# Moving small table steps, two weight loads and one VectorE step inside the first layer norm of a GNN and expert kernel

## The reference

```
def _sage_layer(h, edge_src, edge_dst, deg_inv, W_self, W_neigh, b):
    msg = h[edge_src]
    agg = segment_sum(msg, edge_dst, num_segments=h.shape[0])
    mean = agg * deg_inv[:, None]
    return h @ W_self + mean @ W_neigh + b

def gnn(x):                       # x is already layer-normed
    h = relu(_sage_layer(x, ..., W_self0, W_neigh0, b0))
    return _sage_layer(h, ..., W_self1, W_neigh1, b1)

def ffn(t):                       # t is already layer-normed
    logits = silu(t @ rw1 + rb1) @ rw2 + rb2          # 8 experts
    w = softmax(top 2 of logits, the rest -inf)
    eh = silu(einsum('td,edh->teh', t, ew1) + eb1)    # hidden size 256
    return t + einsum('te,ted->td', w, einsum('teh,ehd->ted', eh, ew2) + eb2)

x = x + gnn(layernorm(x))
x = x + ffn(layernorm(x))
```

## Time and profile before

| | |
|---|---|
| median of 3 runs | 1164.46 us (1163.42 to 1165.69) |
| the profiled execution, its own time | 1165.69 us |
| its span (first to last instruction) | 1163.9 us |
| PE busy | 1083.5 us, 93% |
| DVE busy | 627.1 us, 54% |
| ACT busy | 434.5 us, 37% |
| POOL busy | 177.0 us, 15% |
| PE on the chain that ended last | 75% of the span |

### The profile page before, as it was taken

How to read it: one execution, slowest core, us unless ns; L and a number is a source line. 1 busy time by engine, 2 the same in 40 slices (tenths; PEclk the granted TensorE clock), 3 DMA queues, 4 the chain that set the end, 5 groups by cost and what they waited for, 6 DMA issues and landing times.

```text
span 1163.9 us, 18112 instructions
## 1 busy us (share of the span) xinstructions
PE 1083.5 (93%) x6504; PEld 1025.4 (88%) x6504; DVE 627.1 (54%) x1099; ACT 434.5 (37%) x936; POOL 177.0 (15%) x199
## 2 busy tenths in 40 slices
PE   4999999999989999999999999999993699999984
PEld 3999999999989999999999999999993598888883
DVE  6578888888452542234224432642215567777752
ACT  5554434444111221121211121643322556667651
POOL 5500000000000020002000200024511223443211
PEclk9999999999999999999999999999996699999977
DMA  7332223321328530033003401765641779999963
GB/s 190 82 103 76 64 68 104 103 72 60 106 57 246 161 101 1 1 128 95 1 1 127 119 1 36 228 195 160 187 172 42 275 245 307 263 271 254 243 173 55
DMA packets 73659, 150.45 MB, mean 129 GB/s; under 512 B 12347, under 2 KB 51192, under 8 KB 69074
## 3 DMA queue, kind: packets, MB, share of 16 engines
q1 hardware_dynamic: 61041, 112.50, 31.0%
q0 software_dynamic: 11840, 36.22, 12.5%
q10 hardware_dynamic: 672, 0.32, 0.1%
HBM read 109.97 MB, written 44.53 MB: 133 GB/s over the span
## 4 chain that ended last, share of the span: by engine, by line
PE 75%; DVE 7%; DMA 5%; issue 4%; ACT 3%; PEld 2%; DVEq 1%; ACTq 1%; POOL 0%; POOLq 0%; SPq 0%; PEldq 0%
PE ps L1459 19%; PE ps L936 14%; PE ps L1531 9%; PE ps L1498 8%; PE ps L1190 7%; PE ps L2087 5%; DMA out<-o_rows,to_i 4%; PE ps L808 4%; PE ps L2103 2%; DVE w_lo L2169 2%; PE ps L2073 1%; ACT w_hi L2123 1%; PEld ps L732 1%; DVE o_rows L2191 1%; PE ps L904 1%
## 5 line engine op out<-in xcount | busy, mean ns | idle before, releaser
L1421 POOL TENSOR_TENSOR s_rows<-s_rows,b1t 125x1368 f32<-125x1368 f32 (+3 forms) x9 | 23.1, 2584 | 584.1 <-DMA s_rows<-in_x 584.1
L815 DVE TENSOR_TENSOR adj<-ps,adj 125x250 f32 x212 | 88.2, 416 | 41.7 <-PE ps L808 33.3
L936 PE MATMUL ps<-h_lo,w_hi 128*128 128x418 f32 x336 | 108.6, 372 | 0.0
L936 PE MATMUL ps<-h_hi,w_hi 128*128 128x418 f32 x336 | 100.3, 379 | 0.0
L1498 PE MATMUL ps<-z_lo,adj 125*125 125x342 f32 (+1 forms) x300 | 95.4, 323 | 2.3 <-issue 2.3
L1498 PE MATMUL ps<-z_hi,adj 125*125 125x342 f32 (+1 forms) x300 | 96.0, 325 | 1.6 <-DVE s_rows L1730 1.6
L936 PE MATMUL ps<-h_hi,w_lo 128*128 128x418 f32 x336 | 93.4, 359 | 0.0
L2087 PE MATMUL ps<-xt_hi,w_hi 128*128 128x256 f32 (+1 forms) x272 | 83.0, 305 | 10.4 <-DVE w_lo L2169 8.9
L1190 PE MATMUL ps<-adj,y_hi 125*128 125x416 f32 (+1 forms) x240 | 86.8, 362 | 4.0 <-issue 3.4
L2169 DVE TENSOR_TENSOR w_lo<-w_raw,w_hi 128x2048 fp32r<-128x2048 f32 x34 | 76.5, 2289 | 21.0 <-ACT w_hi L2123 19.6
L1190 PE MATMUL ps<-adj,y_lo 125*128 125x416 f32 (+1 forms) x240 | 86.5, 360 | 1.1 <-issue 1.1
(11 more groups left out here) (302 smaller groups left out, 2700.6 us busy)
## 6 DMA issues: line engine op xcount, KB each, us to landing
w_raw<-in_L_ffn_ew SPq DMA_DIRECT2D x34, 1024.0 KB, 7.1
xin<-in_x SPq DMA_DIRECT2D x10, 448.0 KB
t_d<-xn SPq DMA_DIRECT2D x10, 448.0 KB
base<-x_d POOLq DMA_DIRECT2D x10, 448.0 KB, 4.1
out<-base POOLq DMA_DIRECT2D x10, 448.0 KB, 3.4
y_d<-y_hi SPq DMA_DIRECT2D x7, 625.0 KB
y_d<-y_lo SPq DMA_DIRECT2D x7, 625.0 KB
self_d<-self SPq DMA_DIRECT2D x7, 625.0 KB
```

Source lines behind the costliest of these rows:

```text
L815: e.tensor_tensor(cols, ps[0:P, 5 + b % 2, 0:KW].rearrange("p (t w) -> p t w", t=NT), cols, ALU.add).then_inc(self.took, 1)
L936: mm = e.matmul(BANK(m, own, c), wt[:, own, k, :], ht[:, k, a:a + w], start=(k == 0 and p == 0), stop=(k == KT - 1 and p == 2))
L1421: e.tensor_tensor(cols, cols, b1t[:, 0:w].rearrange("p (a n) -> p a n", a=1).to_broadcast([P, n, w]), ALU.add).then_inc(s_x, 1)
```

## The change

Four edits, all in the layer norm's stage:

```
-            if i == 2:
+            if i == 4:
                 e.wait_ge(s_iota, 9)
                 e.wait_ge(s_ecast, 3)
                 e.matmul(ps[0:NW, 2, 480:481], earlier[:], col[0:NW, 4:5], ...)     # L478
-            if i == 4:
+            if i == 8:
                 e.wait_ge(s_ecast, 4)
                 e.matmul(ps[0:NW, 2, 488:489], differ[:], col[0:NW, 6:7], ...)      # L481

-        TABLES = {1: runs_table, 3: first_table, 6: past_table, 11: falls_table}
+        TABLES = {1: runs_table, 6: first_table, 8: past_table, 11: falls_table}

                 for i in range(NT):                     # SP
                     load(i)
-                    if i == 4:
+                    if i == 3:
                         e.dma_start(w_raw[:, 0, :, :], view(I["L0_gnn_W_neigh0"])...)
+                    if i == 6:
+                        e.dma_start(w_raw[:, 1, :, :], view(I["L0_gnn_W_self0"])...)
                     if i == 7:
-                        e.dma_start(w_raw[:, 1, :, :], view(I["L0_gnn_W_self0"])...)
-                    if i == 8:
                         e.dma_start(d_seq[:], ...)      # and the two loads of d_next

-                for t in along((0, moments), (1, inverse), (DEEP, low(0)), (0, spread), (1, shift), (DEEP, low(1))):
+                for t in along((DEEP, low(0)), (0, moments), (1, inverse), (0, spread), (1, shift), (DEEP, low(1))):

                 for t in along((DEEP, high), (0, deviation), (1, normal)):      # ACT
-                    if t == 4:
+                    if t == 3:
                         slab_high(e, 0, l0_win[0], 16, l0_wok[0])
-                    if t == 7:
+                    if t == 6:
                         e.wait_ge(s_ecast, 2)
                         slab_high(e, 1, l0_win[1], 16, l0_wok[1])
```

More of the change, by code:

```diff
@@ L618, in _ @@
                     load(i)
-                    if i == 4:
+                    if i == 3:
                         e.dma_start(w_raw[:, 0, :, :], view(I["L0_gnn_W_neigh0"])[:, :, 0:128]).then_inc(l0_win[0], 16)
+                    if i == 6:
+                        e.dma_start(w_raw[:, 1, :, :], view(I["L0_gnn_W_self0"])[:, :, 0:128]).then_inc(l0_win[1], 16)
                     if i == 7:
-                        e.dma_start(w_raw[:, 1, :, :], view(I["L0_gnn_W_self0"])[:, :, 0:128]).then_inc(l0_win[1], 16)
-                    if i == 8:
                         e.dma_start(d_seq[:], I["dst"].rearrange("(p n) -> p n", p=P)).then_inc(s_seq, 16)
```

## The result

The changed kernel is slower: 1174.66 us median (1171.35 to 1177.68) against 1163.42 for the kernel before (1161.82 to 1165.69), five runs each, ratio 1.0092 with a 95% interval of [1.0065, 1.0117]. A second series, of four and seven runs, gave 1174.44 against 1160.10, ratio 1.0112 [1.0089, 1.0136]. These ratios are worked out from the single runs; the two medians of a series alone would give 1.0097 and 1.0124. The forecast was 1175.5, in a range of 1170 to 1181. The profiled execution took 1172.83 us, with a span of 1171.0.

What follows compares the result with a forecast made beforehand. Until 29.87 us the loop of DVE and ACT bounds, afterwards PE. 4.54 - 0.77 + 0.38 + 4.99 + 1.5 + 0.4 = 11.0 us on the profiled 1165.69, less 1.23, gave 1175.5 us, range 1170.0 to 1181.0.

Steps and rivals of the forecast that it cites:

- The ring: DVE's moments behind low part and h_hi, ACT's next h_hi behind them: lap 4.08 us from 2.76, first product 4.54 later.
- Slab 1's hole: PE's wait at 37.52 for POOL's low part of slab 1, before turn 6's product, closes: gain 0.77 us.
- Early loads: Slab loads and roundings one step earlier: loading slab 0 put at no cost, with 0 to 0.5 us carried.
- Turn 8: PE reaches this turn of its stream at 47.22 instead of 43.07, 4.15 us later.
- the 0.4 put down for turn 4: Extra slow PE pace in turn 4, from a longer pause behind tile 4's transposes: 0.4 us, up to 1.8 possible.
- PE's wait for tile 7: PE comes to tile 7's transposes at 43.69, before its xn allows them at 44.07: 0.38 us wait.
- The stop: In turn 8 PE waits behind L481 for past table, moments, shift and xn: 4.99 us until tile 8's transposes.
- The clock: PE's clock falls in the stop behind L481; slow transposes and matmuls cost 1.5 us, bounds 0 and 6.8.
- Only the ring bites: Rival: the past table's trip in step 8 is hidden; 4.15 + 0.4 us, about 1169; chance 0.05.
- A clock that stays low for 13 us behind the stop: Rival: after turn 8's stop the clock stays low as in 1116 to 1130; about 1180 us; chance 0.15.
- the third rival: Late stage's clock, 1116 to 1130, falls out otherwise: about 1170.2 or 1181 us; chance 0.15, two thirds low.

Runs made afterwards that it cites:

- the step 9 version: Changed kernel with the past table on DVE in step 9 instead of 8, PE's order as in the changed kernel; ratio 1.0050 to the kernel before.
- The ring alone: Kernel before with only the low part of bank 0 put ahead of the moments in DVE's list; ratio 1.0059 to the kernel before.

## Why the prediction was right

- *The ring.* Forecast lap 4.08 us, measured 4.07 and 4.09. First product forecast for 34.41, measured 34.24; with the order alone, and no table or load moved, 33.96. One link is not the one that binds, without effect on the sum: the prediction has ACT's xn wait for the shift, and in the trace it is the square root ahead of it that waits last, for the aggregate of the next tile.
- *Slab 1's hole.* Forecast gain 0.77; turns 5, 6 and 7 now start 3.16 and 3.13 us apart and nothing waits for POOL. Early loads cost nothing, as put.
- *Turn 8.* Forecast to begin at 47.22, and at 47.62 with the 0.4 put down for turn 4; measured 47.62. That it fits to the hundredth is luck: the first product came 0.17 us sooner, turn 4 took 0.88 us more where 0.38 and 0.4 were forecast (PE's wait for tile 7 did not show, because PE came later than it), and in the second profile turns 4 and 5 took 0.6 us more again.
- *The stop.* Forecast 4.99 us from turn 8's start to its transposes, measured 4.93. That it comes from the place of the table on DVE is shown by the step 9 version (0.17 us left); that it does not need the ring, by the version with the order undone (4.61).
- *The clock.* This is the mis-sized term. Forecast were 1.5 us behind the stop, taken from the start of the kernel before: 0.91 for the transposes and 0.58 for the twelve matmuls. Measured were 5.80 - 3.24 = 2.6 (2.5 to 2.7 by the experiment that kept PE busy). Of it 0.82 is the transposes, and 1.74 the twelve matmuls and what follows up to L485. The model had only the first four of the twelve at slow pace, as in turn 4 of the kernel before; here it was the first eleven.
- *What the price goes by.* Read in quarters of a microsecond, the granted clock was at 0.5 from 51.2 to 58.0 in the changed kernel, from 52.1 to 59.0 in its second profile, from 46.6 to 53.4 with the order undone and from 44.4 to 51.3 with the tables alone. Of these stretches 5.5, 6.2, 6.2 and 3.8 us lie behind the start of tile 8's transposes, and the prices are 2.6, 2.8, 2.8 and 1.8. So the price is near half of what is left of the low stretch when PE's work comes back, and not a matter of the stop's length alone. With the tables alone the stop was the longest, the clock fell 3.1 us ahead of its end, and the price was the smallest.
- *The sum.* 11.0 forecast, 12.2 and 13.1 at the mark, 10.7 and 13.0 by the ratios (0.0092 and 0.0112 of 1162). The ring alone is 5.2, the tables alone 6.6, the loads alone -0.5; together 11.3, so they add up to within 0.9 and 1.8 us. That the median came within 0.9 us of the forecast is in part luck: the clock's term was 1.1 too small, and single runs of the changed kernel lie 6 us apart.
- *The rivals.* "Only the ring bites" is what two experiments give (+5) once the table is out of the way. A clock that stays low for 13 us behind the stop did not come: it was 6.8. The late stages, which the third rival is about, took from 1097.3 to 1103.6 us in the eleven profiles, and no experiment tells what moves them.
- The Trainium skill ("TensorE: Matmul & The Clock Gate", "What's actually happening") states the warm-up as a span of time and not a number of matmuls. The prediction took from it that every stop would cost alike. That does not follow: the same section also says that the number of slow matmuls changes from run to run. The traces agree with that: the price behind the stop in turn 8 was 2.6 and 2.8 in two profiles of the same kernel, and 1.8 with the tables alone.

What stays open: why turn 4 takes 3.86 us in one profile of the changed kernel and 4.31 in the other, and anything from 2.98 to 4.32 among the kernels with DVE's old order.

## What to carry to other kernels

In this kernel the table step was 1.0 us of work and cost 4.9 us of waiting and 2.6 of slow pace. A small step in an engine's list costs little by itself; what counts is what stands behind it while it waits. Before moving a step that two engines hand to and fro, look at both lists: the asker must come to it after the giver has passed it, and nothing that the giver itself needs next may stand behind the asker's wait. And a piece of work that fills the time in which its engine waits for another should stay ahead of that wait: moved behind it, it becomes part of the loop.

## What the runs showed of the hardware

- A DVE tensor_scalar of 50x212 took 1.39 us instead of 0.32 and ended 0.13 us behind the end of POOL's memsets. One of 1x212 took 1.24 or 1.25 us in all eleven profiles and ended 0.11 to 0.13 us behind the end of others.
- A stop of 4.68 us cost 2.5 to 2.7 us more behind it through PE's clock, and matmuls that computed nothing of use, put into the stop, took this away. After the like stops of 4.61 and 5.67 us it was 2.8 and 1.8.
- In turn 4 matmuls started 0.35 us apart while the clock column showed 1.00; the same matmuls start 0.19 apart later.
